# Query gates with six product slots, accumulating DMAs, a third addition on GpSimd, and hand-placed folds and sums

## The chip, the cores and the metric

One core of one Trainium2 chip runs the whole kernel in one launch. The metric is the device time of the launch in microseconds. The kernel before takes 818.7 us (median of three runs, 816.2 to 818.98).

## The reference

A graph of 256 nodes with 768 features passes through two gated relational graph convolutions, three more relational convolutions, and a tail of graph attention and a small MLP. The change touches the two gates, one after each of the first two convolutions. With `h3` of shape (8, 32, 768) and queries `q` of shape (8, 64, 768) a gate is:

```python
hg = jnp.einsum('bnf,gf->bng', h3, Wg[:, :F])
qg = jnp.einsum('blf,gf->blg', q, Wg[:, F:]) + bg
attn = jax.nn.sigmoid(hg[:, :, None, :] + qg[:, None, :, :])
qi = jnp.einsum('bnlf,blf->bnf', attn, q)
alpha = jax.nn.sigmoid(jnp.einsum('bnf,gf->bng', h3, Wq[:, :F]) + jnp.einsum('bnf,gf->bng', qi, Wq[:, F:]) + bq)
hn = alpha * jnp.tanh(qi) + (1.0 - alpha) * h3
```

So 8 x 32 x 64 x 768 sigmoids are made, multiplied by the queries and summed over the 64 tokens of each graph.

## The kernel before

Each gate is a loop of 48 steps (`STEPS`), one per pair of a feature chunk of 128 and a graph. The features lie on the partitions, and a step has 32 nodes x 64 tokens = 2048 numbers per partition. Steps 0 to 23 (`HALF`) are graphs 0 to 3, steps 24 to 47 graphs 4 to 7; within a half the chunk `f` advances every four steps.

One step passes through the engines so:

- **TensorE** (L1389, `arguments`) makes the sigmoid arguments of the upper 32 tokens (u = 1) and the lower 32 (u = 0) in two pairs of PSUM banks. Each waits until ScalarE has read the same half of the step before.
- **ScalarE** (L810, `sigmoid`) writes the sigmoids of each half into a slot of `prod`. There are `PSLOTS` = 4 slots, and the tokens of a node are adjacent in one. The upper half may be overwritten once the first addition of the step four earlier is done; the lower half once its TensorE fold has read it, or VectorE has reduced it.
- **VectorE** (L1995, `gate_product`) multiplies the 2048 numbers by the query values, which lie in PSUM bank 6.
- **GpSimd** (L593, `fold`) adds the upper 32 tokens to the lower 32, in all steps but the last. Then the steps differ by `KIND`: at "pool" steps GpSimd also adds 16 to 16 (L596); at "tensor" steps TensorE folds 32 to 4 by eight accumulating identity products into bank 7 (L1436, run at the step that `FOLD_AT` lists, three steps later); "vector" steps (`ALONE`) get nothing more.
- **VectorE** (L2013, `reduce`) sums what is left, 4, 16 or 32 tokens per node, into `qi_t`. Its place is two or three steps later (`REST_AT`), in order of the steps.

The first gate has 13 tensor, 22 pool and 12 vector steps, the second 16, 23 and 8. Step 47 is reduced whole, from 2048 numbers.

Around these stands other work, whose order is written out by step number in every engine's program. TensorE runs `beside(s)` behind the arguments of step s: projections and, in steps 24 to 47, the products with W_q. `query_part(1, m0, m1)` needs `qi_t` of the second half; its products m = 8 and 9 (chunk 4) wait at L1377 until the 44 steps 0 to 43 are reduced. In both gates they stand in `beside(47)`. A `fold(s)` of the same step comes behind them. After step 47 TensorE transposes chunks 0 to 4 of `qi_t`, runs 16 products of the next layer's root weights (`root`), waits for all 48 reduces, transposes chunk 5 and runs the last two products m = 10 and 11. Alpha, the state and the next layer hang on those. Every instruction of an engine is run in its order, so a wait holds up all that is behind it. SyncE's queue carries the weight loads into a ring of four (`w_raw`) and the spreads of head and query rows into `h_and_q`; GpSimd's program issues no DMA.

```python
KIND = [[kind_of(i, s) for s in range(STEPS - 1)] for i in range(2)]
REST_AT = [[s + (3 if KIND[i][s] == "tensor" and KIND[i][s + 1] != "tensor" else 2) for s in range(STEPS - 1)] for i in range(2)]
                    elif i == 0 and s in (42, 43):
                        query_part(1, 3 * (s - 42), 3 * (s - 42) + 3)
                    elif i == 0 and s in (45, 47):
                        query_part(1, s - 39, s - 37)
                    if s in FOLD_AT[i]:
                        fold(s)
```

## Time and profile before

| what | value |
|---|---|
| timed runs, median (lowest to highest) | 818.7 us (816.2 to 818.98) |
| profiled execution, first to last instruction | 814.7 us |
| profiled span against the median of the runs | 4.0 us shorter |
| TensorE's granted clock over the span | full speed in all 40 slices |
| busy over the span: TensorE / VectorE / GpSimd / ScalarE | 771.4 / 605.2 / 517.8 / 424.9 us |
| first gate, first product to end of product 47 | 116.85 to 261.07 us |
| second gate, the same | 332.34 to 477.73 us |

For the profiled execution only the span is given and no device time of its own, so a sum made on the span is carried to the median by the difference in the third row. Busy shares over the whole span mix stages with different limits; the gates are 290 us of it. In timeline rows the columns are start, duration, engine, line, operation, and in brackets the idle time ahead of the first instruction and what ended it; "x3" says that instructions that follow each other were merged.

### The profile page before, as it was taken

Reading aid. Unit: us, or ns where it says so; the run is one execution under the profiler, and the core shown is the slowest. Engines: PE = TensorE matmul, PEld = TensorE weight load, DVE = VectorE, ACT = ScalarE, POOL = GpSimd, SP = SyncE. Lnnn points to the kernel's source line nnn. Section 1 sums busy time; section 2 is a strip of 40 time slices with the busy share of each in tenths; the row PEclk is TensorE's granted clock in tenths of the full one; section 3 lists DMA queues with packets and bytes.
Section 4 is the critical chain, followed back from the end, with each engine's and each line's share of the span. In section 5 each row is a group of like instructions: output and inputs, shape, how many; then the busy total and the mean of one; then the engine's idle time right before and its main releaser. Section 6 shows DMA issues by size and latency. Waiting matters only on the chain.

```text
span 814.7 us, 10588 instructions
## 1 busy us (share of the span) xinstructions
PE 771.4 (95%) x4195; PEld 640.1 (79%) x4198; DVE 605.2 (74%) x664; ACT 424.9 (52%) x508; POOL 517.8 (64%) x221
## 2 busy tenths in 40 slices
PE   7999999999988999998898889999999999998998
PEld 4669986776645699776666558999999999976897
DVE  8966249999999640889999997764696488666454
ACT  6424446777674342677676725434443444253742
POOL 0625619999998284699999955770685178805500
PEclk9999999999999999999999999999999999999999
DMA  9037526445332464270153328556356546350001
GB/s 365 33 82 234 164 71 176 91 141 156 116 117 78 122 232 150 58 201 1 63 195 117 116 79 281 185 194 230 108 166 207 181 131 218 117 233 0 2 1 39
DMA packets 24409, 111.01 MB, mean 136 GB/s; under 512 B 3620, under 2 KB 6180, under 8 KB 23976
## 3 DMA queue, kind: packets, MB, share of 16 engines
q1 hardware_dynamic: 23240, 104.24, 39.7%
q10 hardware_dynamic: 1120, 6.10, 2.0%
q8 instruction: 33, 0.54, 0.3%
q14 instruction: 16, 0.13, 0.0%
HBM read 100.63 MB, written 0.79 MB: 124 GB/s over the span
## 4 chain that ended last, share of the span: by engine, by line
PE 62%; DVE 19%; POOL 13%; ACT 3%; issue 2%; DMA 0%; DVEq 0%; ACTq 0%
PE ps L1098 28%; DVE prod L1995 11%; POOL prod L593 8%; PE ps L1064 8%; PE ps L1129 5%; DVE qi_t L2013 4%; PE ps L1611 3%; POOL prod L596 2%; PE ps L1389 2%; PE ps L1256 2%; PE ps L1277 2%; PE ps L1679 1%; PE ps L1436 1%; PE ps L1257 1%; PE ps L1326 1%
## 5 line engine op out<-in xcount | busy, mean ns | idle before, releaser
L581 POOL TENSOR_TENSOR w_lo<-w_raw,w_hi 128x1536 fp32r<-128x1536 f32 x49 | 183.7, 3762 | 141.1 <-ACT w_hi L677 141.0
L593 POOL TENSOR_TENSOR prod<-prod 128x1024 f32<-128x1024 f32 x94 | 223.1, 2396 | 26.8 <-DVE prod L1995 26.6
L810 ACT ACTIVATE prod<-ps 128x1024 f32<-128x1024 f32 x192 | 187.4, 1023 | 68.6 <-PE ps L1389 56.0
L1995 DVE TENSOR_TENSOR prod<-prod,ps 128x2048 f32<-128x2048 f32 x96 | 217.7, 2279 | 5.5 <-ACT prod L810 3.5
L677 ACT ACTIVATE w_hi<-w_raw 128x1536 fp32r<-128x1536 f32 x60 | 88.9, 1488 | 119.1 <-PE ps L1098 108.7
L1389 PE MATMUL ps<-sel_pair,h_and_q 128*128 128x512 f32 x384 | 128.2, 446 | 16.7 <-ACT prod L810 16.5
L1098 PE MATMUL ps<-w_hi,yt_hi 128*128 128x384 f32 x480 | 122.9, 336 | 0.1
L1098 PE MATMUL ps<-w_lo,yt_hi 128*128 128x384 f32 x480 | 121.9, 334 | 0.0
L1098 PE MATMUL ps<-w_hi,yt_lo 128*128 128x384 f32 x480 | 121.8, 334 | 0.0
L1389 PEld LDWEIGHTS ps<-sel_pair,h_and_q 128*128 128x128 f32 x384 | 66.5, 189 | 52.5 <-ACT prod L810 32.3
L1064 PE MATMUL ps<-w_raw,h_t 128*128 128x384 f32 x312 | 106.5, 486 | 0.0
L1098 PEld LDWEIGHTS ps<-w_lo,yt_hi 128*128 128x128 f32 x480 | 86.8, 188 | 0.0
L1098 PEld LDWEIGHTS ps<-w_hi,yt_lo 128*128 128x128 f32 x480 | 86.7, 188 | 0.0
L1098 PEld LDWEIGHTS ps<-w_hi,yt_hi 128*128 128x128 f32 x480 | 85.4, 188 | 0.9 <-POOL w_lo L581 0.9
L1064 PEld LDWEIGHTS ps<-w_raw,h_t 128*128 128x128 f32 x312 | 58.8, 189 | 34.3
L1883 DVE TENSOR_TENSOR ps<-ps,rinv 128x512 f32<-128x512 f32 x54 | 36.7, 695 | 56.1 <-PE ps L1129 55.5
L1436 PEld LDWEIGHTS ps<-prod,ident 128*128 128x128 f32 x464 | 55.2, 191 | 14.4 <-DVE qi_t L2013 7.8
L1436 PE MATMUL ps<-prod,ident 128*128 128x128 f32 x464 | 57.5, 277 | 7.9 <-POOL prod L593 7.9
L596 POOL TENSOR_TENSOR prod<-prod 128x512 f32<-128x512 f32 x45 | 58.2, 1294 | 3.5
L2013 DVE TENSOR_REDUCE qi_t<-prod 128x32 f32<-128x512 f32 (+1 forms) x67 | 58.9, 884 | 1.2 <-POOL prod L596 1.0
L677 ACT ACTIVATE yt_hi<-ps 128x512 fp32r<-128x512 f32 (+1 forms) x58 | 35.0, 612 | 40.8 <-DVE ps L1883 40.5
L1870 DVE TENSOR_TENSOR w_lo<-w_raw,w_hi 128x1536 fp32r<-128x1536 f32 x11 | 20.1, 1828 | 44.4 <-ACT w_hi L677 44.4
(260 smaller groups left out, 1104.4 us busy)
## 6 DMA issues: line engine op xcount, KB each, us to landing
w_raw<-weights SPq DMA_DIRECT2D x105, 768.0 KB, 4.4
wa_in<-weights SPq DMA_DIRECT2D x6, 768.0 KB, 5.9
w_gat<-weights SPq DMA_DIRECT2D x6, 768.0 KB, 7.9
w_query<-weights SPq DMA_DIRECT2D x3, 768.0 KB, 11.6
h_and_q<-stage_hi SPq DMA_DIRECT2D x24, 96.0 KB, 2.1
h_and_q<-stage_lo SPq DMA_DIRECT2D x24, 96.0 KB, 2.2
a_vec<-gat_vectors ACTq DMA_DIRECT2D x1, 2048.0 KB, 9.6
q_t<-queries ACTq DMA_DIRECT2D x1, 1536.0 KB, 10.5
```

The costliest lines, as they stand in the source:

```text
L581: pool.tensor_tensor(Wl[:, j, :], raw_slab(U, 0, j), Wh[:, j, :], ALU.subtract).then_inc(w_lo_by_pool, 1)
L593: pool.tensor_tensor(v[:, :, 0:32], v[:, :, 0:32], v[:, :, 32:64], ALU.add).then_inc(folded_once, 1)
L596: pool.tensor_tensor(v[:, :, 0:16], v[:, :, 0:16], v[:, :, 16:32], ALU.add).then_inc(folded_twice, 1)
L677: return act.activation(o, i, ACT.Copy)
L810: act.activation(slot_view(s)[:, :, 32 * u:32 * u + 32], args.rearrange("p b (n l) -> p (b n) l", l=LH), ACT.Sigmoid).then_inc(sigmoid_rea ...
L1064: return pe.matmul(ps[:, bank + h, 0:FH], left, raw_slab(U, c, k // 2)[:, o:o + FH], start=start, stop=stop)
L1098: mm = pe.matmul(ps[:, bank + h, 0:FH], Y[:, s, k, t * P:(t + 1) * P], Wx[:, j, c0:c0 + FH], start=False, stop=(last and k == KC - 1 and n ...
L1129: ins = pe.matmul(ps[:, 4 + j, kk * N:(kk + 1) * N], Hx[:, t, k * P:(k + 1) * P], A[:, t, v - 1, :], start=(n == 0), stop=(n == 3))
L1389: mm = pe.matmul(ps[:, bank + h, :], HQ[:, b, u, f * P:(f + 1) * P], SEL[:, h * 512:(h + 1) * 512], start=True, stop=True)
L1436: mm = pe.matmul(o, ident[:], slot_view(s)[:, :, 4 * k:4 * k + 4], start=(k == 0), stop=(k == 7))
L1995: TT(slot_view(s), slot_view(s), ps[:, 6, o:o + L].unsqueeze(1).broadcast_to([P, NB, L]), ALU.mult).then_inc(products_ready, 1)
L2013: dve.tensor_reduce(qiT[:, f, b * NB:(b + 1) * NB], terms, AX.X, ALU.add).then_inc(qi_ready, 1)
```

## The change

In the gates a slot becomes two contiguous halves of 32 x 32 numbers (upper and lower tokens), and there are six slots instead of four. The sixth lies over buffers of the hidden state's split, the fifth reaches over part of `yt_hi`; for that `h_t` moves by 6144 bytes and the two halves of `yt_hi`/`yt_lo` change their turns (`1 - v % 2`, and index 1 for the root). The attention tail uses a second name, `HA`, for the old place of `h_t`; in all its lines only the name changes.

The first addition of 33 of the 94 steps (`BY_DMA`: 16 and 17) becomes a DMA with addition, 4096 bytes per partition, issued by GpSimd at the place where it would have added. There are four kinds now: T (TensorE folds 32 to 4), G (a second addition on GpSimd), H (new: a second and a third addition on GpSimd, 8 tokens left for VectorE), V (nothing more). The first gate has 12 T, 11 G, 13 H, 11 V, the second 15, 11, 11, 10. Where each fold, second addition and reduce stands is listed by step in `FOLD_AT`, `SECOND_AT` and `REST_AT`; reduces no longer come in the order of the steps. The waits on `qi_ready` are worked out from the lists (`reduced`), and mean the same steps as before.

```diff
-PSLOTS = 4
+PSLOTS = 6
...
-FOLD_AT = [(5, 8, 11, 14, 15, 17, 20, 22, 23, 26, 35, 44, 46),
-           (5, 8, 9, 11, 12, 14, 15, 17, 18, 20, 21, 23, 26, 35, 38, 41)]
-ALONE = [(4, 10, 16, 25, 27, 28, 30, 34, 37, 40, 42, 45), (25, 27, 28, 30, 34, 40, 42, 44)]
-
-
-def kind_of(i, s):
-    if s + 3 in FOLD_AT[i]:
-        return "tensor"
-    return "vector" if s in ALONE[i] else "pool"
-
-
-KIND = [[kind_of(i, s) for s in range(STEPS - 1)] for i in range(2)]
-REST_AT = [[s + (3 if KIND[i][s] == "tensor" and KIND[i][s + 1] != "tensor" else 2) for s in range(STEPS - 1)] for i in range(2)]
+KIND = ["HVGHVTGTHVTHTGGTVGTHHVGTVHGHGTHTVVHGTVVGHTGHVTH",
+        "VGHVGTTHTGTHVTHGVTTHGVVTHGTVGGTHTGVTTHVHGTVGTHH"]
+BY_DMA = [(1, 10, 12, 15, 19, 21, 23, 24, 30, 32, 34, 35, 36, 38, 41, 44),
+          (3, 8, 10, 13, 16, 19, 21, 24, 26, 27, 31, 34, 36, 38, 41, 42, 44)]
+FOLD_AT = [{8: 5, 11: 7, 15: 10, 17: 12, 20: 15, 22: 18, 28: 23, 34: 29, 35: 31, 41: 36, 46: 41, 47: 45},
+           {8: 5, 11: 6, 13: 8, 15: 10, 18: 13, 21: 17, 23: 18, 26: 23, 31: 26, 35: 30, 36: 32, 38: 35, 41: 36, 46: 41, 47:
+           44}]
+SECOND_AT = [[(0,), (), (2,), (3,), (), (), (6,), (), (8,), (), (), (11,), (), (13,), (14,), (), (), (17,), (), (), (20,),
+             (19,), (22,), (), (), (25,), (26,), (27,), (28,), (), (), (), (), (), (30,), (), (34,), (35,), (), (39,), (40,),
+             (), (42,), (43,), (), (), (46,)],
+             [(), (1,), (2,), (), (4,), (), (), (7,), (), (9,), (), (11,), (), (), (14,), (15,), (), (), (), (), (20,),
+             (19,), (), (), (), (25,), (24,), (), (28,), (29,), (), (), (), (33,), (31,), (), (), (37,), (), (39,), (40,),
+             (), (), (43,), (), (45,), (46,)]]
+REST_AT = [[(), (), (0,), (), (1,), (), (2, 4), (3,), (6,), (5,), (8,), (7, 9), (), (), (), (10, 11, 13), (14,), (12,), (),
+           (16,), (15,), (17,), (), (18, 19, 20), (), (21, 22), (), (), (23, 24, 25, 26), (), (), (27, 28), (), (), (29,),
+           (30, 31, 32), (33,), (), (34,), (35, 37), (), (36, 38), (39, 40), (), (), (), (41,), (42, 43), (44, 45, 46)],
+           [(), (), (0,), (), (1,), (), (2, 4), (3,), (5,), (), (7,), (6,), (), (8, 9), (11,), (10, 12), (), (), (13, 14),
+           (), (15, 16), (17,), (), (18, 20), (19, 22), (21,), (23,), (25,), (24,), (), (), (26, 27, 28, 29), (), (), (),
+           (30,), (31, 32), (33, 34), (), (35, 37), (), (36, 38, 39), (), (40,), (), (43,), (41, 42), (45,), (44, 46)]]
+
+
+def numbered(keys):
+
+    return {s: n + 1 for n, s in enumerate(keys)}
+
+
+FIRST_BY_POOL = [numbered(s for s in range(STEPS - 1) if s not in BY_DMA[i]) for i in range(2)]
+DMA_BEFORE = [sum(s % PSLOTS == k for s in BY_DMA[0]) for k in range(PSLOTS)]
+SECOND = [numbered(s for at in SECOND_AT[i] for s in at) for i in range(2)]
+THIRD = [numbered(s for s in SECOND[i] if KIND[i][s] == "H") for i in range(2)]
+FOLDED = [numbered(FOLD_AT[i].values()) for i in range(2)]
+REDUCED = [numbered([s for at in REST_AT[i][:STEPS] for s in at] + [STEPS - 1] + list(REST_AT[i][STEPS])) for i in range(2)]
 QUERY_EVENTS = [0, 1, 5, 6]
 HEAD_EVENTS = [(2, 3, 4), (7, 8, 9)]
-BANK7 = [sorted([(s, "fold", s - 3) for s in FOLD_AT[0]] + [(29, "q", 0), (32, "q", 1), (38, "h", 0), (40, "h", 1)]),
-         sorted([(s, "fold", s - 3) for s in FOLD_AT[1]] + [(29, "q", 0), (32, "q", 1), (43, "h", 0), (45, "h", 1)])]
+BANK7 = [sorted([(at, "fold", s) for at, s in FOLD_AT[0].items()] + [(29, "q", 0), (32, "q", 1), (38, "h", 0), (40, "h", 1)]),
...
-        PR = sb("prod", [P, PSLOTS, 2048], F32, wh_off)
-        HT = sb("h_t", [P, KC, N], F32, y_off)
+        HT = sb("h_t", [P, KC, N], F32, y_off + 6144)
+        HA = sb("h_t_attention", [P, KC, N], F32, y_off)
...
+        PR = [sb(f"prod{k}", [P, 2, NB, LH], F32, wh_off + 8192 * k if k < 5 else g_off + 16384) for k in range(PSLOTS)]
...
-            return PR[:, s % PSLOTS, :].rearrange("p (n l) -> p n l", l=L)
+            return PR[s % PSLOTS][:]
 
         def place_of(s):
 
             t, f, bb = s // HALF, (s % HALF) // 4, s % 4
             return t, f, 4 * t + bb, bb
 
-        def count_kind(i, s, kind):
-
-            return sum(k == kind for g in range(i) for k in KIND[g]) + sum(k == kind for k in KIND[i][:s + 1])
+        def wait_folded(eng, i, s):
+
+            if s in BY_DMA[i]:
+                k = s % PSLOTS
+                before = DMA_BEFORE[k] if i == 1 else 0
+                eng.wait_ge(dma_folded[k], 16 * (before + sum(q % PSLOTS == k and q <= s for q in BY_DMA[i])))
+            else:
+                eng.wait_ge(folded_once, (len(FIRST_BY_POOL[0]) if i == 1 else 0) + FIRST_BY_POOL[i][s])
+
+        def second(i, s):
+
+            return (len(SECOND[0]) if i == 1 else 0) + SECOND[i][s]
+
+        def third(i, s):
+
+            return (len(THIRD[0]) if i == 1 else 0) + THIRD[i][s]
+
+        def by_tensor(i, s):
+
+            return (len(FOLDED[0]) if i == 1 else 0) + FOLDED[i][s]
+
+        def reduced(i, steps):
+
+            return STEPS * i + max(REDUCED[i][s] for s in steps)
...
-            def fold(i, s):
+            def first_fold(i, s):
 
                 v = slot_view(s)
                 pool.wait_ge(products_ready, STEPS * i + (s + 1))
-                pool.tensor_tensor(v[:, :, 0:32], v[:, :, 0:32], v[:, :, 32:64], ALU.add).then_inc(folded_once, 1)
-                if KIND[i][s] == "pool":
-                    pool.wait_ge(folded_once, (STEPS - 1) * i + (s + 1))
-                    pool.tensor_tensor(v[:, :, 0:16], v[:, :, 0:16], v[:, :, 16:32], ALU.add).then_inc(folded_twice, 1)
-
+                if s in BY_DMA[i]:
+                    pool.dma_start(v[:, 0].rearrange("p n l -> p (n l)"), v[:, 1].rearrange("p n l -> p (n l)"),
+                                   accum_op=ALU.add).then_inc(dma_folded[s % PSLOTS], 16)
+                else:
+                    pool.tensor_tensor(v[:, 0], v[:, 0], v[:, 1], ALU.add).then_inc(folded_once, 1)
+
+            def second_fold(i, s):
+
+                v = slot_view(s)[:, 0]
+                wait_folded(pool, i, s)
+                pool.tensor_tensor(v[:, :, 0:16], v[:, :, 0:16], v[:, :, 16:32], ALU.add).then_inc(folded_twice, 1)
+                if KIND[i][s] == "H":
+                    pool.wait_ge(folded_twice, second(i, s))
+                    pool.tensor_tensor(v[:, :, 0:8], v[:, :, 0:8], v[:, :, 8:16], ALU.add).then_inc(folded_thrice, 1)
 
             def gate_add(i):
 
@@ -642,7 +694,9 @@
                         pool.wait_ge(h_ready[t], 2 * i + 2)
                         pool.tensor_tensor(X[:, t, :], X[:, t, :], H[:, t, :], ALU.add).then_inc(state_added, 1)
                 for s in range(STEPS - 1):
-                    fold(i, s)
+                    first_fold(i, s)
+                    for q in SECOND_AT[i][s]:
+                        second_fold(i, q)
...
-                    copy(YTh[:, v % 2, 2 * j:2 * j + 2, :], tile3(j)).then_inc(yt_hi_ready, 1)
+                    copy(YTh[:, 1 - v % 2, 2 * j:2 * j + 2, :], tile3(j)).then_inc(yt_hi_ready, 1)
...
-                            act.wait_ge(folded_once, (STEPS - 1) * i + (s - PSLOTS + 1))
-                        elif KIND[i][s - PSLOTS] == "tensor":
-                            act.wait_ge(fold_ready, count_kind(i, s - PSLOTS, "tensor"))
+                            wait_folded(act, i, s - PSLOTS)
+                        elif KIND[i][s - PSLOTS] == "T":
+                            act.wait_ge(fold_ready, by_tensor(i, s - PSLOTS))
                         else:
-                            act.wait_ge(qi_ready, STEPS * i + (s - PSLOTS + 1))
+                            act.wait_ge(qi_ready, reduced(i, [s - PSLOTS]))
                     args = ps[:, (4 if u else pair(i, 1)):(6 if u else pair(i, 1) + 2), :]
-                    act.activation(slot_view(s)[:, :, 32 * u:32 * u + 32],
+                    act.activation(slot_view(s)[:, u],
...
-                            pe.wait_ge(qi_ready, STEPS * i + HALF + 4 * f + 4)
+                            pe.wait_ge(qi_ready, reduced(i, range(HALF + 4 * f + 4)))
...
-                    s = at_ - 3
+                    s = FOLD_AT[i][at_]
                     bank7_free(at_)
-                    pe.wait_ge(folded_once, (STEPS - 1) * i + (s + 1))
+                    wait_folded(pe, i, s)
                     o = ps[:, 7, 0:4 * NB].rearrange("p (n l) -> p n l", l=4)
                     for k in range(8):
-                        mm = pe.matmul(o, ident[:], slot_view(s)[:, :, 4 * k:4 * k + 4], start=(k == 0), stop=(k == 7))
+                        mm = pe.matmul(o, ident[:], slot_view(s)[:, 0, :, 4 * k:4 * k + 4], start=(k == 0), stop=(k == 7))
...
-                    pe.wait_ge(qi_ready, STEPS * i + HALF)
+                    pe.wait_ge(qi_ready, reduced(i, range(HALF)))
...
-                    TT(slot_view(s), slot_view(s), ps[:, 6, o:o + L].unsqueeze(1).broadcast_to([P, NB, L]),
-                       ALU.mult).then_inc(products_ready, 1)
+                    query = ps[:, 6, o:o + L].rearrange("p (u l) -> p u l", u=2).unsqueeze(2).broadcast_to([P, 2, NB, LH])
+                    TT(slot_view(s), slot_view(s), query, ALU.mult).then_inc(products_ready, 1)
 
                 def reduce(s):
 
                     _, f, b, _ = place_of(s)
                     if s == STEPS - 1:
                         dve.wait_ge(products_ready, STEPS * (i + 1))
-                        terms = slot_view(s)
-                    elif KIND[i][s] == "tensor":
-                        dve.wait_ge(fold_ready, count_kind(i, s, "tensor"))
+                        dve.tensor_reduce(qiT[:, f, b * NB:(b + 1) * NB], slot_view(s).rearrange("p u n l -> p n u l"),
+                                          AX.XY, ALU.add).then_inc(qi_ready, 1)
+                        return
+                    if KIND[i][s] == "T":
+                        dve.wait_ge(fold_ready, by_tensor(i, s))
                         terms = ps[:, 7, 0:4 * NB].rearrange("p (n l) -> p n l", l=4)
-                    elif KIND[i][s] == "pool":
-                        dve.wait_ge(folded_twice, count_kind(i, s, "pool"))
-                        terms = slot_view(s)[:, :, 0:16]
+                    elif KIND[i][s] == "H":
+                        dve.wait_ge(folded_thrice, third(i, s))
+                        terms = slot_view(s)[:, 0, :, 0:8]
+                    elif KIND[i][s] == "G":
+                        dve.wait_ge(folded_twice, second(i, s))
+                        terms = slot_view(s)[:, 0, :, 0:16]
                     else:
-                        dve.wait_ge(folded_once, (STEPS - 1) * i + (s + 1))
-                        terms = slot_view(s)[:, :, 0:32]
+                        wait_folded(dve, i, s)
+                        terms = slot_view(s)[:, 0]
...
-                    for past in (s - 3, s - 2):
-                        if past >= 0 and REST_AT[i][past] == s:
-                            reduce(past)
+                    for past in REST_AT[i][s]:
+                        reduce(past)
...
                 reduce(STEPS - 1)
-                reduce(STEPS - 2)
+                for past in REST_AT[i][STEPS]:
+                    reduce(past)
```

## Rows read from the trace of the kernel before

**Rows 1.** Stretches from first product to end of product 47, one row per gate

```profile
core 0: us, PE busy (x) PEld busy (x) DVE busy (x) ACT busy (x) POOL busy (x), PEclk, DMA share, GB/s
116.85:261.07 144.22, 133.06 (x604) 94.68 (x604) 140.18 (x102) 100.86 (x111) 139.01 (x69) 1.00 0.43 125
332.34:477.73 145.39, 129.14 (x608) 90.72 (x608) 138.54 (x105) 101.12 (x111) 140.20 (x71) 1.00 0.36 111
```

**Rows 2.** VectorE by line and form, 114 to 258.5 us: count, busy us, mean ns

```profile
L1995 DVE TENSOR_TENSOR prod<-prod,ps 128x2048 f32<-128x2048 f32 x47 | 106.4, 2278 | 2.5 <-ACT prod L810 1.4 <-ACT ps L677 1.0
L2013 DVE TENSOR_REDUCE qi_t<-prod 128x32 f32<-128x512 f32 x21 | 14.2, 678 | 0.9 <-POOL prod L596 0.7
L2013 DVE TENSOR_REDUCE qi_t<-prod 128x32 f32<-128x1024 f32 x11 | 13.3, 1211 | 0.0
L2013 DVE TENSOR_REDUCE qi_t<-ps 128x32 f32<-128x128 f32 x13 | 3.7, 284 | 0.6 <-PE ps L1436 0.6
```

**Rows 3.** GpSimd by line and form, 114 to 258.5 us

```profile
L593 POOL TENSOR_TENSOR prod<-prod 128x1024 f32<-128x1024 f32 x46 | 109.2, 2399 | 20.9 <-DVE prod L1995 20.8
L596 POOL TENSOR_TENSOR prod<-prod 128x512 f32<-128x512 f32 x21 | 27.3, 1298 | 1.6
L603 POOL TENSOR_TENSOR h<-h,tanh_q 128x768 f32<-128x768 f32 x1 | 1.8, 1829 | 0.0
```

**Rows 4.** Timeline of VectorE, steps 0 to 8 of the first gate, step 7 of the second

```profile
116.85 2.29 DVE L1995 TENSOR_TENSOR prod<-prod,ps 128x2048 f32<-128x2048 f32 x1
...
134.42 2.28 DVE L1995 TENSOR_TENSOR prod<-prod,ps 128x2048 f32<-128x2048 f32 x1
136.62 1.21 DVE L2013 TENSOR_REDUCE qi_t<-prod 128x32 f32<-128x1024 f32 x1
137.75 2.28 DVE L1995 TENSOR_TENSOR prod<-prod,ps 128x2048 f32<-128x2048 f32 x1
139.94 0.95 DVE L1921 TENSOR_TENSOR stage_lo<-ps,stage_hi 128x768 fp32r<-128x768 f32 x1
141.89 2.29 DVE L1995 TENSOR_TENSOR prod<-prod,ps 128x2048 f32<-128x2048 f32 x1 [1.00 <-ACT ps L677]
...
356.92 0.29 DVE L2013 TENSOR_REDUCE qi_t<-ps 128x32 f32<-128x128 f32 x1 [1.49 <-PE ps L1436]
```

**Rows 5.** Chain of waits, in order of time: a TensorE fold in step 5

```profile
129.88 1.78 PE ps L1436 x16
```

**Rows 6.** Timeline of TensorE and VectorE at the end of the first gate

```profile
258.43 1.53 PE L1064 MATMUL ps<-w_raw,qi_t 128*128 128x384 f32 x4 [1.76 <-DVE qi_t L2013]
258.79 2.28 DVE L1995 TENSOR_TENSOR prod<-prod,ps 128x2048 f32<-128x2048 f32 x1
260.70 5.32 PE L1064 MATMUL ps<-w_raw,h_t 128*128 128x384 f32 x16
260.99 4.00 DVE L2013 TENSOR_REDUCE qi_t<-prod 128x32 f32<-128x1024 f32 x3
265.97 1.46 PE L1064 MATMUL ps<-w_raw,qi_t 128*128 128x384 f32 x4
270.32 0.88 PE L1074 MATMUL ps<-ident,h 128*128 128x128 f32 x6 [0.32 <-DVE h L2042]
```

**Rows 7.** The same at the end of the second gate

```profile
472.36 1.53 PE L1064 MATMUL ps<-w_raw,qi_t 128*128 128x384 f32 x4 [1.02 <-DVE qi_t L2013]
475.45 2.28 DVE L1995 TENSOR_TENSOR prod<-prod,ps 128x2048 f32<-128x2048 f32 x1
481.33 1.46 PE L1064 MATMUL ps<-w_raw,qi_t 128*128 128x384 f32 x4
```

**Rows 8.** DMA issues of the first gate: count, KB each, median us to landing

```profile
w_raw<-weights SPq DMA_DIRECT2D x17, 768.0 KB, 4.4
h_and_q<-stage_hi SPq DMA_DIRECT2D x12, 96.0 KB, 2.1
```

**Rows 9.** Duration of a DMA issue on SyncE's queue, ns (min/median/max)

```profile
L495 SPq DMA_DIRECT2D h_and_q<-stage_hi x8: 512/591/594, 159.8 to 186.6; - x8
```

37 lines of the change are left out of this document (20 added, 17 removed).

## The prediction

> **What bounds the kernel now.** The change is confined to the two gates, so I read first the two stretches from the first product to the end of product 47 [rows 1]. In the first VectorE is busy for 140.2 of 144.2 us, GpSimd for 139.0, TensorE for 133.1; ScalarE has a third of its time free. In the second they stand at 138.5, 140.2 and 129.1 of 145.4. So three engines are within a few per cent of the stretch, and none can be called the bound from its share. What the change can save before product 47 ends is VectorE's work and its idle time: 4.0 us idle in the first gate, 6.9 in the second. Next, VectorE by form [rows 2]: the product is 2278 ns and stays; a reduce costs 1211 ns with 32 tokens left, 678 with 16, 284 with 4. In the timeline [rows 4] each starts 0.08 us before the one ahead ends (134.42 + 2.28 against 136.62; 136.62 + 1.21 against 137.75), so in a row they cost 1.13, 0.60 and 0.20 us. GpSimd by form [rows 3]: a first addition takes 2.40 us, a second 1.30. Last, the end of a gate, where TensorE runs one unbroken chain behind a wait on VectorE's reduces [rows 6, 7]; the next layer hangs on it.
>
> **VectorE before the end of product 47.** A reduce over 8 tokens (256 numbers) isn't in the trace. Its bounds are the 4-token and the 16-token form, 0.20 and 0.60 us; on the line between 128 and 512 numbers it is 0.33, which I take. First gate before: the reduces of steps 45 (V) and 46 (G) come behind product 47, ahead of it stand 11 V, 21 G, 13 T = 12.4 + 12.6 + 2.6 = 27.6 us. After: 42 to 46 come behind it, ahead stand 10 V, 10 G, 11 H, 11 T = 11.3 + 6.0 + 3.6 + 2.2 = 23.1. That is -4.5 us. Second gate: 8 V, 21 G, 16 T = 24.8 before (45 and 46 behind); 10 V, 11 G, 9 H, 14 T = 23.7 after. That is -1.2 (23.67 from 24.84). With H at its bounds, 0.20 or 0.60, these sums move by 1.4 us down or 3.0 us up in the first gate, 1.2 or 2.4 in the second. Product, sigmoid and fold read or write the same counts in another order; I take their durations unchanged.
>
> **VectorE's idle time.** By step 8 the first gate has lost 2.2 us, 1.00 of them at 141.89, behind TensorE's head products and a fold in step 5 that costs 1.78 [rows 4, 5]. The new list has no fold before step 8, in either gate. In the second, VectorE waited 1.49 us at 356.92 for the fold of step 8, since the reduce of step 5 stood in step 7 [rows 4]; it now stands in step 8. Up to step 28 the folds fall from 10 to 7 and from 13 to 8, so TensorE is relieved of 5.3 and 8.9 us there; they come back later, where it has more room. The reduces of steps 7, 15, 23, 31 and 39 now cover the copy of the next query values. Of the idle 4.0 us I keep 1.5, of the 6.9 I keep 2.5. New waits: where a slot is reduced five steps after its product (G or H: step 30 in the first gate, 15 and 31 in the second) the lower sigmoid of the sixth step waits for it, 1.0 us, and behind it VectorE has a reduce of 1.13 us at best. I put 0.4 us for the first, 0.4 and 1.3 for the others. So -2.1 and -2.6 us; bounds: nothing gained, and all of 4.0 and 6.9.
>
> **GpSimd.** First gate: 31 first additions x 2.40, 24 second x 1.30, 13 third, one of 1.83. The third has half the numbers of the second; 2399 and 1298 ns for 1024 and 512 give 0.75. Sum 74.4 + 31.2 + 9.8 + 1.8 = 117.2 us plus 16 DMA issues. Second: 30, 22, 11, and 2.4 of other work (prices as before [rows 3]): 72.0 + 28.6 + 8.3 + 2.4 = 111.3 plus 17. The price p of an issue on GpSimd's queue is not in the trace. The nearest below is SyncE's issue, 0.59 us [rows 9]; above stands the addition that it replaces, 2.40. Behind the first product the stretches have 135.3 and 139.3 us by this sum, so an issue costs nothing until p is about (135.3 - 117.2)/16 = 1.1 us in the first gate and 1.6 in the second. I take p below 1.1, nearer to the row of an issue than to that of an arithmetic instruction, and nothing for it.
>
> The Trainium skill, "DMA: Bandwidth & Descriptors", section "Latency and other measured facts", puts the software path's first byte at about 1 us and blames the writing of descriptors. With p = 1.0 GpSimd would come to 133.2 and 128.3 us, just inside; that no row shows.
>
> **The DMAs.** 33 transfers of 512 KB, 16 and 17 to a gate. Rows bound one by 2.1 us (96 KB) and, if both addends are moved at the rate of a weight load (4.4 us for 768 KB), 6.0 us [rows 8]. The nearest use is GpSimd's own second addition two steps later, at five places (19, 34, 35; 19, 24), or some 5.8 us at 2.9 a step; everything else has three steps or more. The share of the DMA engines, 0.43 and 0.36 at 125 and 111 GB/s [rows 1], rises by 8.4 MB to about 0.63, or 0.83 if they count twice. SyncE's queue holds none of them. I take nothing, and the six slots are what makes that possible.
>
> **The end of each gate: what the change gives back.** TensorE's products m = 8 and 9 wait for the reduces of steps 0 to 43. First gate before: they start at 258.43, 2.64 us ahead of product 47's end at 261.07; from there TensorE works for 9.0 us to 267.43, and the next layer starts 2.9 later [rows 6]. After: reduces 42 and 43 stand in step 47, behind product 47: 0.60 + 0.33 later, so the start is at the end + 0.95. And fold 45, in step 47, lies behind m = 8 and 9 in TensorE's order: +1.8 [rows 5]. So the next layer starts (0.95 + 9.0 + 1.8) - 6.36 = 5.4 us later, counted from product 47's end. VectorE's own rest there, 0.33 + 2.20 + 1.13 + 0.20 + 0.33, is done by +5 us and hides behind TensorE's 16 root products (5.32). Second gate before: start at 472.36, 5.37 us ahead of the end (477.73); the last products end at 482.79, end + 5.1, having waited for the last reduce [rows 7]. After: m = 8 and 9 are released by reduce 42, in step 46, just as product 47 starts, 2.2 ahead; + 9.0 + 1.8 is end + 8.6. That is +3.5.
>
> **Sum:** -4.5 - 2.1 + 5.4 = -1.2 and -1.2 - 2.6 + 3.5 = -0.3; together -1.5 us. The profiled span is 814.7, so 813.2; the median of the runs is 4.0 above the span, 818.7, which gives **817.2**. What a measurement of this kernel tells from no change is about 0.5%, 4.1 us.
>
> **Rivals.**
>
> *VectorE becomes the clean bound.* With six slots and fewer early folds all 10.9 us of idle go: -5.7 - 10.9 + 8.9 = -7.7, **811.0**. For it: the waits that I found are of the kinds that the lists move. Against: every third step still ties ScalarE's slot to a reduce of the step before, and five query copies a gate need the product ahead of them. Chance 0.32.
>
> *The issues are dear, and GpSimd is the bound.* Place: the first gate, steps 0 to 28, where GpSimd has least to spare. It decides from p = 1.1. At p = 1.5 GpSimd needs 117.2 + 24.0 + 2.3 ahead of it + 2 of its own waits = 145.5, against 137.6 for VectorE: +8, so **825**. At 2.4 the gates would take 160 and 156 us, 22 and 14 above the sum: 853, the far end. For it: GpSimd gets 24 third additions on top (18 us) and was at 96%. Against: SyncE's issue. Chance 0.22.
>
> *The transfers are late.* At 9 us each the five near uses hold GpSimd for 3 us apiece, and with it the first additions behind; a third of it shows: +5, **822**. Weight loads would lengthen too. For it: two addends each, three issues in a row at steps 34 to 36. The Trainium skill says in "Collectives: The Full Stack", "The bandwidth ceiling: the fold count and why AG ≠ RS ≠ AR", that an adding transfer reads two sources for one write and runs at half the rate of a copy; that makes this rival likelier than a plain 512 KB would. Against: 11 us or more of cover at most places. Chance 0.10.
>
> **How the numbers follow.** The forecast has 0.36. Faster by over 0.5% holds the first rival, 0.32; within it the forecast, 0.36; slower the two others, 0.32. The range leaves a tenth on each side: down to 810, the first rival with a little of H's lower bound, up to 829, where p is about 1.7. The forecast's own range is 814.5 to 821.
>
> **What would show it.** Right: first product to end of product 47 near 137.6 and 141.6 us; from there to the next layer's start some 14.7 us in the first gate (9.25 before); products m = 8 and 9 waiting for VectorE; 24 reduces of 256 numbers near 0.41 us long; GpSimd with idle time in both gates. Wrong: gaps on GpSimd's row above 1.1 us at each issue and VectorE waiting for its additions; landings over 6 us; or TensorE's end chain starting before product 47 ends in the first gate.

## The result, and the profile after

The changed kernel takes 828.0 us (median of 4 runs, 827.42 to 833.57) against 817.6 for the kernel before beside it: the medians are 10.4 us apart, the measured ratio is 1.0141, 95% interval 1.0121 to 1.016. It is slower; the forecast was 817.2. The profiled span is 826.5 us, 11.8 more than before. A span lies about 1.8 us below the time of its own run (826.5 against 828.33); the 4.0 us by which the forecast carried its sum from span to median were more, since the profiled execution before (814.7) was one of that kernel's shorter ones. Here is where the 11.8 us lie. "Body" is the stretch from the first product of a gate to the end of product 47, "end" the stretch from there to TensorE's first instruction of the next layer (L1128 in the first gate, L1199 in the second):

| us | start | body 1 | end 1 | between | body 2 | end 2 | rest | span |
|---|---|---|---|---|---|---|---|---|
| before | 116.9 | 144.2 | 9.2 | 62.0 | 145.4 | 7.6 | 329.4 | 814.7 |
| after | 116.6 | 141.1 | 17.5 | 62.0 | 147.0 | 13.0 | 329.2 | 826.5 |
| forecast | | 137.6 | 14.6 | | 141.6 | 11.1 | | 813.2 |

The page of the changed kernel, its lines on the engines' busy time, the clock, the accumulating DMAs (queue q0, which the kernel before doesn't use) and the chain that ended last:

```profile
PE 778.5 (94%) x4163; PEld 642.8 (78%) x4166; DVE 598.4 (72%) x664; ACT 423.3 (51%) x508; POOL 487.1 (59%) x246
...
PEclk9999999999998999999999999999999999999999
...
q0 software_dynamic: 4752, 17.30, 11.3%
...
PE 71%; DVE 12%; ACT 5%; DMA 4%; POOL 4%; issue 3%; SPq 1%; DVEq 0%; ACTq 0%
```

VectorE has 6.8 us less work than before (605.2), GpSimd 30.7 less (517.8). The work went away and the time grew: what came is waiting. The transfers are on the chain, with 4%, and TensorE's clock is no longer full in every slice.

The two bodies, as in [rows 1] (windows of the changed kernel; same columns):

```profile
116.61:257.71 141.10, 127.88 (x559) 88.95 (x558) 135.05 (x99) 99.20 (x110) 126.85 (x84) 1.00 0.75 187
337.06:484.24 147.18, 128.32 (x560) 87.83 (x559) 136.44 (x105) 99.83 (x111) 121.54 (x80) 0.96 0.67 170
```

(The second window opens 0.2 us ahead of the first product.) VectorE works 135.05 and 136.44 us, where the terms of the forecast leave 140.2 - 4.5 = 135.7 and 138.5 - 1.2 = 137.3. But it is idle for 6.0 and 10.7 us, where 1.9 and 4.2 had been kept. The first body is shorter than before by less than its saved work; the second is longer, though it has 2.1 us less of it.

VectorE's reduces and GpSimd's forms in the first gate, as in [rows 2, 3] (114 to 255.4 us):

```profile
L2072 DVE TENSOR_REDUCE qi_t<-prod 128x32 f32<-128x1024 f32 x10 | 12.1, 1212 | 0.0
L2072 DVE TENSOR_REDUCE qi_t<-prod 128x32 f32<-128x512 f32 x10 | 6.8, 680 | 0.0
L2072 DVE TENSOR_REDUCE qi_t<-prod 128x32 f32<-128x256 f32 x11 | 4.5, 413 | 0.0
L2072 DVE TENSOR_REDUCE qi_t<-ps 128x32 f32<-128x128 f32 x11 | 3.1, 286 | 0.0
```

```profile
L640 POOL TENSOR_TENSOR prod<-prod 128x1024 f32<-128x1024 f32 x31 | 74.5, 2419 | 25.8 <-DVE prod L2050 25.6
L646 POOL TENSOR_TENSOR prod<-prod 128x512 f32<-128x512 f32 x23 | 30.5, 1325 | 1.5
L637 POOL DMA_DIRECT2D prod<-prod x16 | 14.0, 896 | 3.3 <-DVE prod L2050 3.2
L649 POOL TENSOR_TENSOR prod<-prod 128x256 f32<-128x256 f32 x12 | 8.8, 730 | 0.9
```

A reduce of 256 numbers takes 413 ns, a third addition 730. The issue of a transfer, for which [rows 9] gave only a lower bound, takes 0.87 us on GpSimd's queue (median of all 33; 839 to 1184 ns). GpSimd is idle 14.3 us in the first body (5.2 before): it is no longer as full as VectorE.

**The transfers.** The issues of the changed kernel (110 to 480 us; KB each, median us to landing), then what the tile's view says of the 33 additions, and the pieces of the chain of waits in which a transfer or what follows it stands (start, us, what):

```profile
w_raw<-weights SPq DMA_DIRECT2D x44, 768.0 KB, 4.8
prod<-prod POOLq DMA_DIRECT2D x33, 512.0 KB, 5.7
a_vec<-gat_vectors ACTq DMA_DIRECT2D x1, 2048.0 KB, 13.0
h_and_q<-stage_hi SPq DMA_DIRECT2D x8, 192.0 KB, 4.2
```

```profile
DMA to landing us min/median/max: 4.5/5.7/13.8
```

```profile
242.59 8.19 DMA prod<-prod
...
364.51 8.60 DMA prod<-prod
373.25 3.28 PE ps L1490 x16
...
410.41 13.75 DMA prod<-prod
```

The median lies within the bounds that [rows 8] gave, 2.1 to 6.0 us. Eleven of the 33 take 7.4 us or more, and eight of these harm nothing, since their results are wanted later still. Three land behind the place that wants them, and these are on the chain. Step 41 of the first gate takes 8.2 us (two 768 KB weight loads fly beside it, one after the other), step 8 of the second 8.6 us (beside it fly five of the 192 KB spreads of `h_and_q`), and step 24 of the second, issued 0.1 us ahead of the 2 MB load of `a_vec`, 13.8 us. The waits for them, in the timeline:

```profile
250.91 2.02 PE L1490 MATMUL ps<-prod,ident 128*128 128x128 f32 x16 [1.28 <-DMA prod<-prod]
373.25 3.28 PE L1490 MATMUL ps<-prod,ident 128*128 128x128 f32 x16 [1.76 <-DMA prod<-prod]
424.24 1.27 POOL L646 TENSOR_TENSOR prod<-prod 128x512 f32<-128x512 f32 x1 [5.71 <-DMA prod<-prod]
```

So TensorE stood at the folds of 41 and 8, five steps behind the issue by the lists, only 7.0 us after it (242.59 to 249.63, and 364.51 to 371.49), and GpSimd at its second addition of step 24 after 8.1 us. For that last one GpSimd stands still for 5.7 us with two additions behind it, and VectorE waits 4.0 us for those.

Transfers also delay others. In the first gate, with the transfers of steps 21, 23 and 24 under way, a 96 KB spread of query rows issued at 182.5 us lands after 4.9 us (2.1 for its like before), SyncE's next issues get longer, and TensorE waits for the last of them:

```profile
183.89 1.43 SPq L538 DMA_DIRECT2D h_and_q<-stage_hi  x1
189.55 1.20 PE L1443 MATMUL ps<-sel_pair,h_and_q 128*128 128x512 f32 x4 [0.75 <-DMA h_and_q<-stage_lo]
```

**The ends and the clock.** TensorE and VectorE at the end of the first gate, as in [rows 6] (timeline), and windows of the same stretch (columns as in [rows 1]):

```profile
255.42 2.29 DVE L2050 TENSOR_TENSOR prod<-prod,ps 128x2048 f32<-128x2048 f32 x1 [1.76 <-ACT prod L864]
...
258.78 2.90 PE L1118 MATMUL ps<-w_raw,qi_t 128*128 128x384 f32 x4 [4.90 <-DVE qi_t L2072]
261.47 3.42 PE L1490 MATMUL ps<-prod,ident 128*128 128x128 f32 x16
...
265.62 5.32 PE L1118 MATMUL ps<-w_raw,h_t 128*128 128x384 f32 x16
...
275.24 0.87 PE L1128 MATMUL ps<-ident,h 128*128 128x128 f32 x6 [0.32 <-DVE h L2101]
```

```profile
254.00:258.00 4.00, 0.00 (x0) 0.00 (x0) 2.58 (x2) 1.39 (x2) 3.92 (x3) 0.96 0.53 100
258.00:260.00 2.00, 1.22 (x2) 0.84 (x3) 2.00 (x3) 0.00 (x0) 1.65 (x2) 0.50 0.00 0
260.00:262.00 2.00, 2.00 (x6) 1.21 (x5) 1.95 (x2) 0.00 (x0) 0.00 (x0) 0.50 0.00 0
262.00:264.00 2.00, 2.00 (x11) 2.00 (x11) 0.00 (x0) 0.00 (x0) 0.00 (x0) 0.50 0.00 0
...
372.00:376.00 4.00, 2.75 (x15) 2.79 (x16) 3.88 (x2) 0.55 (x1) 3.84 (x4) 0.72 1.00 194
```

Products m = 8 and 9 start 1.07 us behind the end of product 47 (257.71), as forecast (0.95). But TensorE had then been idle for 4.90 us, and its granted clock stood at half (0.50, 1.2 of 2.4 GHz) until 264.5: the four products took 2.90 us instead of 1.53 and the fold of step 45 took 3.42 instead of the 1.95 of a fold at full clock in the same view. That is the 2.9 us by which this end is longer than forecast. The Trainium skill says in "TensorE: Matmul & The Clock Gate", "Part 1: The HAM clock gate", that the clock of an idle TensorE falls to half and comes back only after it has worked again; this trace agrees. At 372 to 376, where the fold of step 8 had waited for its transfer, the mean clock was 0.72 and the fold took 3.28.

The end of the second gate, as in [rows 7]:

```profile
482.20 2.13 PE L1118 MATMUL ps<-w_raw,qi_t 128*128 128x384 f32 x4 [2.08 <-DVE qi_t L2072]
484.27 3.04 PE L1490 MATMUL ps<-prod,ident 128*128 128x128 f32 x16
...
493.31 1.46 PE L1118 MATMUL ps<-w_raw,qi_t 128*128 128x384 f32 x4
```

Products m = 8 and 9 are released as product 47 starts (481.97), as forecast; here too the clock is down from 483.0 on (2.13 and 3.04 us).

### The profile page after: what moved, and what is told of

Same layout as the page of the kernel before. It is cut to its first block, busy times and chain, and to the rows that moved or that the text cites. A ratio compares the mean times of both kernels' runs of the same rounds, so it can differ in the third digit from the quotient of the medians.

```text
span 826.5 us, 10539 instructions
## 1 busy us (share of the span) xinstructions
PE 778.5 (94%) x4163; PEld 642.8 (78%) x4166; DVE 598.4 (72%) x664; ACT 423.3 (51%) x508; POOL 487.1 (59%) x246
## 3 DMA queue, kind: packets, MB, share of 16 engines
q0 software_dynamic: 4752, 17.30, 11.3%
## 4 chain that ended last, share of the span: by engine, by line
PE 71%; DVE 12%; ACT 5%; DMA 4%; POOL 4%; issue 3%; SPq 1%; DVEq 0%; ACTq 0%
PE ps L1152 27%; PE ps L1118 13%; DVE prod L2050 7%; PE ps L1183 5%; PE ps L1443 5%; PE ps L1490 4%; DMA prod<-prod 4%; PE ps L1665 3%; ACT prod L864 3%; PE ps L1331 2%; PE ps L1310 2%; DVE qi_t L2072 2%; POOL w_lo L624 1%; PE ps L1733 1%; PE ps L1311 1%
## 5 line engine op out<-in xcount | busy, mean ns | idle before, releaser
L640 POOL TENSOR_TENSOR prod<-prod 128x1024 f32<-128x1024 f32 x61 | 146.7, 2418 | 42.8 <-DVE prod L2050 42.3
L646 POOL TENSOR_TENSOR prod<-prod 128x512 f32<-128x512 f32 x46 | 61.2, 1330 | 8.8 <-DMA prod<-prod 5.7
L1490 PEld LDWEIGHTS ps<-prod,ident 128*128 128x128 f32 x432 | 57.3, 208 | 9.3 <-issue 5.8
L2072 DVE TENSOR_REDUCE qi_t<-prod 128x32 f32<-128x256 f32 (+2 forms) x67 | 48.8, 751 | 4.0 <-POOL prod L649 4.0
## 6 DMA issues: line engine op xcount, KB each, us to landing
w_query<-weights SPq DMA_DIRECT2D x3, 768.0 KB, 11.8
```

Source lines behind the costliest of these rows:

```text
L640: pool.tensor_tensor(v[:, 0], v[:, 0], v[:, 1], ALU.add).then_inc(folded_once, 1)
L646: pool.tensor_tensor(v[:, :, 0:16], v[:, :, 0:16], v[:, :, 16:32], ALU.add).then_inc(folded_twice, 1)
L1490: mm = pe.matmul(o, ident[:], slot_view(s)[:, 0, :, 4 * k:4 * k + 4], start=(k == 0), stop=(k == 7))
L2072: dve.tensor_reduce(qiT[:, f, b * NB:(b + 1) * NB], terms, AX.X, ALU.add).then_inc(qi_ready, 1)
```

## The experiments

The theory after the result: the lists do save VectorE's work, and three things give back more than that: the late transfers, the order of work at the ends of the gates, and the half clock that follows on TensorE's waits. The rivals: the slots themselves, the transfers' load on the memory as such, and GpSimd. The twelve runs, each set against the kernel before on its chip (medians of 817.6 to 818.4):

| run | median us | ratio (95%) | body 1 | end 1 | body 2 | end 2 | rest | span |
|---|---|---|---|---|---|---|---|---|
| six_slots | 818.6 | 1.0001 (0.9991 to 1.001) | 144.2 | 9.2 | 145.4 | 7.6 | 329.1 | 814.5 |
| sums_in_46 | 821.2 | 1.0038 (1.0022 to 1.0054) | 141.6 | 10.6 | 143.6 | 13.1 | 329.3 | 817.9 |
| root_first | 822.2 | 1.0052 (1.0032 to 1.0072) | 141.3 | 11.8 | 145.3 | 11.1 | 329.6 | 818.8 |
| vectors_later | 825.5 | 1.0096 (1.0071 to 1.0121) | 141.3 | 16.4 | 142.6 | 13.0 | 330.5 | 823.8 |
| no_dmas | 840.8 | 1.0283 (1.0267 to 1.0299) | 151.6 | 16.2 | 149.1 | 12.9 | 329.3 | 838.4 |
| plain_copies | 819.6 | 1.0035 (1.001 to 1.0059) | 138.8 | 17.0 | 139.0 | 12.9 | 329.6 | 816.1 |
| combined | 819.2 | 1.0008 (0.9995 to 1.0022) | 141.2 | 11.8 | 142.7 | 11.1 | 330.9 | 817.4 |
| fewer_dmas | 813.5 | 0.995 (0.9935 to 0.9966) | 140.5 | 11.2 | 139.7 | 11.1 | 330.6 | 812.2 |
| fewer_alone | 820.1 | 1.0021 (1.0007 to 1.0036) | 139.7 | 17.2 | 139.1 | 12.0 | 329.8 | 817.5 |
| no_last_fold | 812.5 | 0.9921 (0.9897 to 0.9944) | 140.3 | 9.5 | 140.1 | 8.9 | 333.2 | 812.3 |
| early_15 | 814.2 | 0.9942 (0.9921 to 0.9963) | 140.3 | 9.5 | 139.7 | 9.0 | 334.9 | 813.2 |
| vectors_stay | 809.7 | 0.9904 (0.9887 to 0.9922) | 140.2 | 9.5 | 138.9 | 8.9 | 330.6 | 806.8 |

The stages are those of one profiled execution each, and executions of one kernel differ (plain_copies' timed runs lie between 817.6 and 825.2 us; the profiled one took 817.9), so a stage is known less well than a median. The stretch between the gates is 62.0 us in all, and the first product comes between 116.6 and 118.3, so spans differ by up to 1.7 us for that reason alone.

**six_slots:** the six slots of contiguous halves with the lists of the kernel before, no transfers, no third addition.

```diff
-KIND, BY_DMA, FOLD_AT, SECOND_AT, REST_AT as changed
+KIND, FOLD_AT, SECOND_AT, REST_AT as in the kernel before; BY_DMA = [(), ()]
```

> The changed kernel with the lists of the kernel before in the new form: six slots and contiguous halves, no DMA with addition, no third addition, folds and reduces where they stood. If the slots alone take away waits between ScalarE and VectorE, the two gates get 2 to 4 us shorter: 814 to 816 us. Rival: VectorE and GpSimd are full and the waits sit elsewhere, so six slots do nothing: within 1 us of the kernel before (817.6). If the layout costs something it is slower than that.

818.6, every stage as before. The layout and the slots cost nothing and, alone, gain nothing.

**sums_in_46:**

```diff
-REST_AT[0][46:] = (41,), (42, 43), (44, 45, 46)
+REST_AT[0][46:] = (41, 42, 43), (), (44, 45, 46)
```

> The changed kernel with the reduces of steps 42 and 43 of the first gate in step 46, ahead of product 47, where VectorE sat idle for 1.8 us. If the wait of TensorE's products m = 8 and 9 is what the first gate's end costs, they start near 254.6 us and not at 258.8, the granted clock stays at full speed behind them, and the next layer starts near 268.3 and not at 275.2: about 6.9 us less, 821 us. Rival (the end hides behind something else, or GpSimd's additions of step 43 come too late): no change, 828.

821.2. The first end falls from 17.5 to 10.6 us, and the body rises by no more than 0.5. In its timeline TensorE's wait ahead of m = 8 and 9 is 0.72 us, and both that and the fold run at full clock:

```profile
256.08 1.53 PE L1104 MATMUL ps<-w_raw,qi_t 128*128 128x384 f32 x4 [0.72 <-DVE qi_t L2058]
257.44 1.95 PE L1476 MATMUL ps<-prod,ident 128*128 128x128 f32 x16
```

Its second body is also 3.4 us shorter than the changed kernel's, with no edit there: of the late landings only that of step 24 is on its chain (12.7 us), not that of step 8. Step 8 still lands after its place of use (8.7 us against 7.0), but off that chain. So a second body of one and the same list is known to some 3 us only, where transfers are near to being late.

**root_first:** in both gates TensorE works its 16 root products ahead of m = 8 and 9 and of the fold in step 47.

```diff
                 def beside(s):
 
+                    if s == STEPS - 1:
+                        return
...
+                root(i + 1, 0, 0, 4)
+                query_part(1, 8, 10)
+                if STEPS - 1 in FOLD_AT[i]:
+                    fold(STEPS - 1)
                 for f in range(KC):
                     if f == KC - 1:
-                        root(i + 1, 0, 0, 4)
```

> The changed kernel with TensorE's 16 root products ahead of m = 8 and 9 and of the fold of step 47, in both gates. They need no reduce, so they fill the wait. Expected by the theory of the end chain: the next layer starts about 6.2 us earlier behind the first gate (5.4 of the order and the clock's fall gone, less a little) and the last products of the second gate 2.5 us earlier: about 819 us. Rival: the sigmoids of step 47 and the reduces end so late that only the clock's fall goes: 3 to 4 us, 824.

822.2, nearer to the rival. End 1 falls to 11.8, end 2 to 11.1: the products are only moved into the wait, and the last two (m = 10, 11) then hang on the last fold and the last reduce.

**vectors_later:** the 2 MB load of `a_vec` from step 25 of the second gate to behind it.

```diff
-                    if s == 25 and i == 1:
-                        act.dma_start(av[:], gavec.partition_broadcast(P))
...
+            act.dma_start(av[:], gavec.partition_broadcast(P))
             act.dma_start(gb[:], gbias.partition_broadcast(P))
```

> The changed kernel with the 2 MB load of the attention vectors moved from step 25 of the second gate to behind the gate. If that load is what made the transfer of step 24 land after 13.8 us, it lands in 6 to 8 us, GpSimd's wait of 5.7 us for it goes and the second gate gets 3 to 5 us shorter: 823 to 825 us. Rival: transfers with addition are late by themselves beside the weight loads (others took over 8 us without that load): under 1 us, 828.

825.5. The transfer of step 24 lands in 6.6 us instead of 13.8, GpSimd's 5.7 us wait is gone, the second body is 4.4 us shorter (1.1 shorter than that of sums_in_46, which keeps the load in its place).

**no_dmas:** all 94 first additions on GpSimd.

```diff
-BY_DMA = [(1, 10, 12, ...), (3, 8, 10, ...)]
+BY_DMA = [(), ()]
```

> The changed kernel with all 94 first additions on GpSimd, everything else as changed (second and third additions too). GpSimd's work becomes 155.6 and 152.1 us in the gates, with what lies ahead of it 160 and 156 against 141.1 and 147.2: about 28 us slower than the changed kernel, 856 us. Rival, if the transfers cost as much as they save: within 10 us of it, 828 to 838.

840.8: between the two figures expected. Its first body, windows view (columns as in [rows 1]):

```profile
117.23:268.90 151.67, 133.19 (x559) 90.62 (x558) 136.75 (x99) 99.14 (x110) 146.87 (x82) 0.97 0.40 118
```

GpSimd is the bound there (146.9 of 151.7). So the lists with third additions need the transfers: these are worth 12.8 us even as they are.

**plain_copies:** the 33 transfers without their addition; this kernel leaves the lower 32 tokens out of 33 sums.

```diff
                     pool.dma_start(v[:, 0]..., v[:, 1]...,
-                                   accum_op=ALU.add).then_inc(dma_folded[s % PSLOTS], 16)
+                                   ).then_inc(dma_folded[s % PSLOTS], 16)
```

> The changed kernel with the 33 DMAs as plain copies of the upper half onto the lower, without the addition (so in 33 steps of 94 the lower 32 tokens are left out of the sum): same bytes per DMA as written, same places. If the second source is what makes them slow, the median landing falls from 5.7 to about 4 us, their share of the DMA engines' time about halves, and the waits for late transfers shrink: 824 us. Rival: the load beside them is what counts, landing stays near 5.7 us, and the time near 828.

819.6. The page's queue line and the tile's landings:

```profile
q0 software_dynamic: 4752, 17.30, 5.5%
```

```profile
DMA to landing us min/median/max: 2.9/3.6/10.5
```

The same 17.30 MB (by the profile's count) take half of the DMA engines' time (5.5% from 11.3%), and the landing falls from 5.7 to 3.6 us. The two bodies are then 138.8 and 139.0 us, 2.3 and 8.0 us less than with the addition. Expected were 4 us less in all; the median is 8.4 lower. The transfer of step 24 is still late (10.5 us), but alone so.

By the rule of the Trainium skill that the prediction named, from "Collectives: The Full Stack", "The bandwidth ceiling: the fold count and why AG ≠ RS ≠ AR", an adding transfer, there in a collective, has half the rate of a copy; for the engines' time this pair of runs agrees (11.3% against 5.5% for the same bytes); the landing grew less, from 3.6 to 5.7 us.

**combined:** sums_in_46, root_first and vectors_later together.

> The three edits together: reduces 42 and 43 in step 46, the root products first in both gates' ends, the attention vectors loaded behind the second gate. Against the changed kernel the first gave 8.4 us, root products first adds only the second gate's 2.5 to it, the vectors 3.7. If the three are the causes that they seem and add up, it takes 814 to 816 us, a little under the kernel before. Rival: they overlap (the time saved is waited for elsewhere): 819 to 821.

819.2, the rival's figure. The edits at the ends overlap: 11.8 and 11.1 us are what root_first gave alone.

**fewer_dmas:** combined, and three transfers become additions on GpSimd again.

```diff
-BY_DMA[0] with 41, BY_DMA[1] with 8 and 24
+BY_DMA[0] without 41, BY_DMA[1] without 8 and 24
```

> As the combined kernel, and the first additions of step 41 in the first gate and 8 and 24 in the second are done by GpSimd itself and not by a DMA; those are the three transfers that another engine was seen to wait for. GpSimd has 14 and 25 us free in the two gates, an addition costs 2.4 - 0.9 = 1.5 us more. If late transfers are what is left, another 2 to 4 us go: about 812. Rival: other transfers are late in their place, or GpSimd's additions come late: 815 or more.

813.5, faster than both kernels. Taking three of 33 transfers out of combined was worth 5.7 us.

**fewer_alone:** these three by themselves, on the changed kernel.

> The changed kernel, where only the first additions of step 41 (first gate) and of steps 8 and 24 (second gate) go back from the DMA to GpSimd; everything else stays as changed. Theory: the three late landings cost by themselves what they cost beside the other edits, 819.2 - 813.5 = 5.7 us; then 828.0 - 5.7 = 822.3 us, and the clock falls near 373 us and in steps 24 to 27 of the second gate are gone. Rival: the late landings hide behind the other losses as long as these are there; then 825 to 827 us.

820.1, that is 7.9 less than the changed kernel (the ratios, 1.0141 and 1.0021, are 1.2% apart, or 9.8 us): the rival (hidden behind the rest) falls. By itself the step is worth more than in combined; that `a_vec` was already out of step 24's way there fits, but no run shows that this is all of it. Windows of its two bodies and of its first end:

```profile
117.69:257.36 139.67, 127.67 (x559) 89.06 (x558) 135.06 (x99) 99.15 (x110) 125.78 (x83) 1.00 0.72 183
336.56:475.67 139.11, 123.84 (x559) 85.30 (x558) 135.88 (x104) 99.64 (x110) 124.65 (x80) 0.99 0.67 172
...
258.00:260.00 2.00, 1.57 (x3) 1.00 (x4) 2.00 (x2) 0.00 (x0) 1.93 (x1) 0.50 0.18 33
```

VectorE's work is as in the changed kernel, its idle time falls from 6.0 to 4.6 and from 10.7 to 3.2 us. TensorE's clock over the second body rises from 0.96 to 0.99: a part of the gain is the clock that no longer falls behind these waits. The DMA share hardly moves (0.75 to 0.72, and 0.67): it was not the load as such that cost most, but three landings in the wrong places. The first end keeps its half clock and its 17.2 us.

**no_last_fold:** fewer_dmas without the fold in step 47 of either gate.

```diff
-KIND[0][45] = "T", KIND[1][44] = "T"; FOLD_AT with 47: 45 and 47: 44
+KIND[0][45] = "V", KIND[1][44] = "V"; both entries gone
```

> Like fewer_dmas, and TensorE's fold in step 47 is gone from both gates (step 45 of the first and 44 of the second are reduced by VectorE from 32 tokens). Theory: TensorE's chain at the end loses 1.8 us in each gate, VectorE's extra 0.93 us hides behind the root products: 813.5 - 3.6 = 809.9 us, VectorE's 3.8 us wait for the fold is gone. Rival: the last products then wait for VectorE's reduces instead of the fold, so that each gate gains 1 us at most: 811.5 to 812.5 us.

The ends shrink by 1.7 and 2.2 us, as the theory has it, but the median only by 1.0 (812.5; the two intervals overlap) and the span not at all: the rest behind the second gate is 2.6 us longer. The rival's figure came true, but not for its reason. The chain of waits there:

```profile
487.73 5.17 PE ps L1103 x16
492.92 7.07 DMA w_raw<-weights
500.01 1.49 ACT w_hi L717
```

A weight load ends at 500.0, as it did in fewer_dmas (499.9), and the third convolution waits for it, however early the gate ends. The 2 MB of `a_vec`, moved there by vectors_later, are under way beside it; vectors_stay below tests whether they make it slow.

**early_15:** no_last_fold, with two reduces of the second gate one step earlier.

```diff
-REST_AT[1][19:21] = (), (15, 16); REST_AT[1][35:37] = (30,), (31, 32)
+REST_AT[1][19:21] = (15,), (16,); REST_AT[1][35:37] = (30, 31), (32,)
```

> Like no_last_fold, and in the second gate the reduces of steps 15 and 31 stand one step earlier (in steps 19 and 35), so that ScalarE's slot is free before it asks for it. Theory: ScalarE's wait of 3.0 us on the reduce of step 15 goes, with it TensorE's idle time ahead of it and the fall of the granted clock near 392 us (0.72 and 0.85 over 8 us, some 1.7 us of TensorE's time): 1.5 to 3 us less than no_last_fold. Rival: TensorE makes that up later in the gate, where VectorE is the bound: within 0.5 us of no_last_fold, though the clock stays up.

The rival: 814.2, no better than no_last_fold (the intervals overlap). The longest of ScalarE's waits for a reduce falls from 2.4 to 1.0 us and the clock stays full at 388 to 400 (0.86 in no_last_fold), yet the body gains only 0.4 us. The clock's other dip stays (0.57 at 376 to 380; 0.63 in no_last_fold), and the rest behind the gate is 1.7 us longer: TensorE waits 2.98 us for a weight piece at 548.55 and then runs at 0.51 of its clock from 550.0 to 553.5.

**vectors_stay:** no_last_fold with the `a_vec` load back in step 25.

```diff
+                    if s == 25 and i == 1:
+                        act.dma_start(av[:], gavec.partition_broadcast(P))
...
-            act.dma_start(av[:], gavec.partition_broadcast(P))
```

> Like no_last_fold (reduces of steps 42 and 43 of the first gate in step 46, TensorE's root products ahead of m = 8 and 9 in both gates, no fold in step 47, first additions of steps 41 and 8, 24 on GpSimd), but the 2 MB load of the attention vectors stays in step 25 of the second gate, as in both kernels. Theory: behind the second gate that load took the DMA engines from the weights of the next layer (no_last_fold waits 7.1 us for a weight load from 492.9 us on), and this ate what the shorter end of the gate gave; with the load back in the gate the weight lands some 2.5 us sooner: 812.5 - 2.5 = 810.0 us, and no wait for weights on the chain behind the second gate. Rival: the load delays the additions of steps 26 and 27 in the gate by as much: 812 to 813 us.

809.7, the best of all kernels, 1% below the one before (0.9887 to 0.9922). The load lands in 9.5 us in the gate and the body is not longer for it (138.9). Step 24 is no transfer now; those of steps 26 and 27 take 10.1 us beside the load, and of all waits of VectorE only one of 0.48 us is for them. Behind the gate the rest is back at 330.6 and no weight load is on the chain, which shows that the moved load was what delayed it. The end of its first gate:

```profile
254.80 5.00 PE L1104 MATMUL ps<-w_raw,h_t 128*128 128x384 f32 x15
...
262.00 1.46 PE L1104 MATMUL ps<-w_raw,qi_t 128*128 128x384 f32 x4
...
266.35 0.88 PE L1114 MATMUL ps<-ident,h 128*128 128x128 f32 x6 [0.32 <-DVE h L2092]
```

The next layer starts 9.5 us behind product 47, as it did before the change (9.2).

## Why the prediction was wrong

The sum was -1.5 us on the span, the trace has +11.8. The miss of 13.3 us is +3.5 and +5.4 in the bodies, +2.9 and +2.0 at the ends, and -0.4 in start and rest (rounded).

**What held.** VectorE's work ahead of product 47's end: 135.1 and 136.3 us against 135.7 and 137.3. The reduce of 256 numbers 0.41 us long (0.33 in a row), the third addition 0.73 (0.75 taken). The issue of a transfer, 0.87 us, below the 1.1 from which it counts; GpSimd idle in both gates. The ends: m = 8 and 9 behind product 47 in the first gate, at its start in the second, the fold in step 47 in the chain. The prediction had worked out +5.4 and +3.5 us for that, and sums_in_46, root_first and no_last_fold each take the part away that their step names.

**The step that failed first: "I take nothing" for the DMAs.** It set one landing against the steps until use, and the landing was within its bounds at the median (5.7 us). Two things in that were wrong. First, the cover: it counted 2.9 us for every step of the lists, so 14.5 us for the folds of 41 and 8, five steps on. The trace has 7.0 for both, and no more than 10.2 for eleven of the twelve transfers whose fold stands five steps on (14.5 for the twelfth, which is behind the stall on step 24). For these GpSimd issues 0.3 to 3.6 us behind the product, and TensorE works off its step well ahead of VectorE's product of the same step (it stood at the fold of step 8, in step 13, when VectorE began product 12). Second, the landing: 8.2, 8.6 and 13.8 us for the three that came late, and each has its company in the list of issues: two weight loads, the spreads of `h_and_q` in the first steps of a gate, the 2 MB load in step 25. The prediction had [rows 8] for the spreads and the ring, but it never laid the due times of other queues beside the 33 issues, and didn't mention the `a_vec` load. Of its own signs of being wrong, "landings over 6 us" came true. fewer_alone prices it: 7.9 us in the median, 9.0 on the span, 1.4 in the first body and 7.9 in the second. With the three gone the bodies are 139.7 and 139.1 us, together 0.4 short of the forecast's 279.2; that is luck, since the first is 2.1 above its forecast and the second 2.5 below.

**The rival "the transfers are late"** named the mechanism and had 0.10. Of the five near uses it counted, one (step 24) was late; the other two late ones were among those that it gave "11 us or more of cover". It put 5 us on it, with landings of 9 us each; the three cost about 8.

**The step that was not there at all: TensorE's clock.** The prediction let TensorE's chain at the end run at the rows of before (1.53, 1.78, 5.32 us), which are rows at full clock, and didn't ask what the new wait ahead of it does. Within an idle time of 4.90 us the clock fell to half and stayed there for 6.8 us: +2.9 in the first gate, and, with a shorter fall, most of the +2.0 in the second (0.6 for the products, 1.1 for the fold). fewer_alone keeps this idle time and the long end (17.2 us), sums_in_46 takes it away and the end goes with it: 6.9 us for a move of two reduces. The prediction's own terms explain some 4 of these, the waiting; the other 2.9 are the clock. No run takes the half clock away and leaves the wait, so the split rests on the durations at either clock.

**VectorE's idle time.** Of 4.0 and 6.9 us 1.5 and 2.5 were kept, and 0.4 and 1.7 added for new waits. Without the late landings (fewer_alone) the second gate has 3.2 against 4.2, the first 4.6 against 1.9. Where those 2.7 us in the first gate come from is settled in part: plain_copies has 0.9 us less of body and lacks VectorE's wait of 0.67 us at 198.6, which comes behind the delayed spreads of query rows; the longest in fewer_alone, 1.22 us at 221.1, stands in plain_copies too, and no run takes it away. ScalarE's wait for the reduce of step 15 in the second gate, put at 1.0 us with 0.4 of it on VectorE, is 3.0, but early_15 shows that little hangs on it.

**The other rivals.** VectorE as the clean bound (0.32): the least idle time in a body is the 2.9 us of vectors_stay's second. Dear issues (0.22): 0.87 us; no_dmas shows what GpSimd as the bound looks like, with 146.9 of 151.7 us busy. A longer weight load, 4.4 us before and 4.8 after, wasn't on the chain in the gates; the delayed spreads of query rows at 187 us were.
